# The router's high rows written by ACT straight from x3, the full rows by DVE, in a two-layer gated transformer kernel

## The reference

```python
x = x + jnp.tanh(g_xattn[0]) * _L0_xattn_ref(_layernorm(x), ctx_2048)            # fp8-like product
x = x + jnp.tanh(g_ffn[0]) * _L0_ffn_ref(_layernorm(x), L0_ffn_weight, ...)      # ternary weights
x = x + jnp.tanh(g_xattn[1]) * _L1_xattn_ref(_layernorm(x), ctx_2048, ctx_2048)  # 8 heads, softmax
x = x + jnp.tanh(g_ffn[1]) * _L1_ffn_ref(_layernorm(x), router_w, Wa, Wb)        # 8 experts, top 2
```

## Time and profile before

| | us |
|---|---|
| median of 3 runs | 2216.24 (2215.17 to 2216.98) |
| the profiled execution, its own time | 2218.67 |
| its span, first to last instruction | 2216.9 |
| PE busy | 1866.9 (84%) |
| DVE busy | 1668.4 (75%) |
| ACT busy | 1360.1 (61%) |
| POOL busy | 858.3 (39%) |

### The profile page before, as it was taken

How to read it: one execution, slowest core, us unless ns; L and a number is a source line. 1 busy time by engine, 2 the same in 40 slices (tenths; PEclk the granted TensorE clock), 3 DMA queues, 4 the chain that set the end, 5 groups by cost and what they waited for, 6 DMA issues and landing times.

```text
span 2216.9 us, 26479 instructions
## 1 busy us (share of the span) xinstructions
PE 1866.9 (84%) x8716; PEld 826.1 (37%) x8716; DVE 1668.4 (75%) x2348; ACT 1360.1 (61%) x2587; POOL 858.3 (39%) x1256
## 2 busy tenths in 40 slices
PE   0186667777746999999999999999999999999997
PEld 0032223332312444444444444444444444444443
DVE  8999989999546777777767777777777767777661
ACT  5798969977225565565565565565565565565650
POOL 2666646654023333333333433333333333433320
PEclk9998887898967999999999999999999999999998
DMA  7778769978637778878888878788778878778781
GB/s 217 193 208 198 199 176 233 250 182 213 183 92 140 150 154 170 159 156 168 158 156 165 161 162 163 158 162 161 161 155 168 158 156 163 164 163 163 133 150 41
DMA packets 963529, 369.33 MB, mean 167 GB/s; under 512 B 915136, under 2 KB 931520, under 8 KB 963392
## 3 DMA queue, kind: packets, MB, share of 16 engines
q1 hardware_dynamic: 963392, 367.64, 76.7%
HBM read 105.42 MB, written 33.55 MB: 63 GB/s over the span
## 4 chain that ended last, share of the span: by engine, by line
DVE 38%; issue 17%; ACT 16%; PE 13%; POOL 9%; DMA 6%; SPq 1%; POOLq 0%; ACTq 0%; DVEq 0%
ACT slot L716 7%; DVE tiny L971 7%; DVE tiny L1240 7%; POOL tiny L572 4%; ACT arena L708 4%; DMA slot<-slot 3%; POOL tiny L570 3%; DVE slot L1244 3%; ACT tiny L702 2%; PE accs L848 2%; PE sc L865 2%; PE accs L850 2%; PE accs L849 2%; DMA probs<-slot 2%; DVE slot L1022 2%
## 5 line engine op out<-in xcount | busy, mean ns | idle before, releaser
L1244 DVE SCALAR_TENSOR_TENSOR slot<-arena,tiny,slot 128x1024 f16<-128x1024 f32 x256 | 328.2, 1282 | 283.2 <-ACT slot L716 283.1
L865 PE MATMUL sc<-arena,slot 128*128 128x512 f16 x1536 | 381.3, 385 | 31.0 <-ACT arena L708 21.3
L716 ACT ACTIVATE slot<-arena,tiny 128x1024 f16<-128x1024 f32 x256 | 293.7, 1147 | 182.0 <-POOL tiny L572 166.6
L570 POOL TENSOR_SCALAR tiny<-tiny 128x1 f32<-128x1 f32 x256 | 99.3, 388 | 704.5 <-ACT arena L708 704.5
L1240 DVE TENSOR_REDUCE tiny<-sc 128x1 f32<-128x1024 f32 x256 | 308.5, 1206 | 57.8 <-PE sc L865 57.8
L708 ACT ACTIVATE arena<-sc,tiny,head_tab 128x1024 f32<-128x1024 f32 x256 | 308.4, 1205 | 8.6
L702 ACT ACTIVATE tiny<-tiny,head_tab 128x1 f32<-128x1 f32 x256 | 74.1, 289 | 359.4 <-DVE tiny L1240 358.4
L810 PE MATMUL sc<-probs,slot 128*128 128x512 f16 x768 | 190.0, 412 | 89.1 <-DMA slot<-slot 78.9
L865 PEld LDWEIGHTS sc<-arena,slot 128*128 128x128 f16 x1536 | 151.2, 99 | 219.7 <-ACT arena L708 25.9
L810 PE MATMUL sc<-wa_hi,slot 128*128 128x512 f16 x512 | 145.8, 406 | 78.1 <-DMA wa_lo<-wb_lo 46.8
L848 PE MATMUL accs<-wb_hi,slot 128*128 128x512 f16 x512 | 195.1, 381 | 7.5 <-DMA slot<-slot 7.5
(11 more groups left out here) (178 smaller groups left out, 3181.0 us busy)
## 6 DMA issues: line engine op xcount, KB each, us to landing
wb_hi<-in_ctx SPq DMA_DIRECT2D x36, 512.0 KB, 4.7
arena<-in_x SPq DMA_DIRECT2D x32, 512.0 KB, 3.6
x_scratch<-arena SPq DMA_DIRECT2D x32, 512.0 KB, 3.1
slot<-x_scratch SPq DMA_DIRECT2D x32, 512.0 KB, 3.8
slot<-in_ctx SPq DMA_DIRECT2D x32, 512.0 KB, 4.1
out<-arena SPq DMA_DIRECT2D x32, 512.0 KB, 3.4
slot<-in_L_ffn_weight SPq DMA_DIRECT2D x16, 512.0 KB, 3.4
slot<-in_L_ffn_Wa SPq DMA_DIRECT2D x16, 512.0 KB, 4.8
```

Source lines behind the costliest of these rows:

```text
L716: act.activation(PH[c % 2], PF[c % 2], ACT.Identity, scale=rinv[c % 2][:]).then_inc(s_ph.sem, 1)
L865: mm = pe.matmul(sc[:, c % 2, h * HALF:(h + 1) * HALF], q[i][:, c * P:(c + 1) * P], k[j][:, h * HALF:(h + 1) * HALF], start=start, stop=stop)
L1244: dve.scalar_tensor_tensor(out=PL[c % 2], in0=PF[c % 2], scalar=rinv[c % 2][:], in1=PH[c % 2], op0=ALU.mult, op1=ALU.subtract).then_inc(s_ ...
```

## The change

`rows_full` moves from ACT to DVE. There it waits for two of POOL's three factors (it subtracts the mean mv4 itself and multiplies by rs4, so it needs no nb4) and for `hidden_low` of the tile before, which reads T4. `rows_high` on ACT no longer copies T4: it reads x3 itself, with nb4 as bias and rs4 as scale, and writes float16. It waits for all three factors and for the transposed hidden rows of the tile before. `rows_low` waits for both. In ACT's order rows_high stands ahead of exp 2, where the two instructions stood behind it; in DVE's order rows_full stands behind row_maxima 2 and rows_low ahead of row_maxima 3.

```diff
@@ ACT @@
-            def rows_full(n):
-                act.wait_ge(l4_p.sem, l4_p.at(n))
-                act.activation(T4[:], X3[n % 2], ACT.Identity, bias=nb4[:], scale=rs4[:]).then_inc(l4_t.sem, 1)
-
             def rows_high(n):
-                act.wait_ge(l4_t.sem, l4_t.at(n))
+                act.wait_ge(l4_p.sem, l4_p.at(n))
                 after(act, h_turned, n - 1)
-                act.copy(T4HL[0], T4[:]).then_inc(l4_hi.sem, 1)
+                act.activation(T4HL[0], X3[n % 2], ACT.Identity, bias=nb4[:], scale=rs4[:]).then_inc(l4_hi.sem, 1)
@@ ACT's order @@
                 if nxt:
                     query_high(n + 1)
+                if prev:
+                    rows_high(n - 1)
                 if cur:
                     exp(n, 2)
-                if prev:
-                    rows_full(n - 1)
-                    rows_high(n - 1)
-                if cur:
                     prob_high(n, 2)
@@ DVE @@
+            def rows_full(n):
+                dve.wait_ge(l4_p.sem, l4_p.at(n, 2))
+                after(dve, h_lo, n - 1)
+                dve.tensor_scalar(T4[:], X3[n % 2], mv4[:, 0:1], rs4[:], ALU.subtract, ALU.mult).then_inc(l4_t.sem, 1)
+
             def rows_low(n):
                 dve.wait_ge(l4_hi.sem, l4_hi.at(n))
+                dve.wait_ge(l4_t.sem, l4_t.at(n))
                 dve.tensor_tensor(T4HL[1], T4[:], T4HL[0], ALU.subtract).then_inc(l4_lo.sem, 1)
@@ DVE's order @@
                 if cur:
                     row_maxima(n, 2)
+                if prev:
+                    rows_full(n - 1)
                 if before:
                     finish_x4(n - 2, 0)
+                if prev:
+                    rows_low(n - 1)
                 if cur:
                     row_maxima(n, 3)
-                if prev:
-                    rows_low(n - 1)
-                if cur:
                     prob_low(n, 2)
```

More of the change, by code:

```diff
@@ L726, in query_high, with rows_high @@
                 act.copy(QHL[n % 2][0], T3[:]).then_inc(l3_hi.sem, 1)
-            def rows_full(n):
+            def rows_high(n):
                 act.wait_ge(l4_p.sem, l4_p.at(n))
-                act.activation(T4[:], X3[n % 2], ACT.Identity, bias=nb4[:], scale=rs4[:]).then_inc(l4_t.sem, 1)
-            def rows_high(n):
-                act.wait_ge(l4_t.sem, l4_t.at(n))
                 after(act, h_turned, n - 1)
-                act.copy(T4HL[0], T4[:]).then_inc(l4_hi.sem, 1)
+                act.activation(T4HL[0], X3[n % 2], ACT.Identity, bias=nb4[:], scale=rs4[:]).then_inc(l4_hi.sem, 1)
             def router_exp(n):
@@ L1331, in _ @@
                     row_maxima(n, 2)
+                if prev:
+                    rows_full(n - 1)
                 if before:
                     finish_x4(n - 2, 0)
-                if cur:
-                    row_maxima(n, 3)
                 if prev:
@@ L1338, in _ @@
                 if cur:
+                    row_maxima(n, 3)
                     prob_low(n, 2)
```

## The result

The changed kernel took 2234.82 us (median of 4 runs, 2232.81 to 2235.55) beside 2216.61 for the kernel before: a ratio of 1.0087 (95% interval 1.0073 to 1.0100), 18 us or 0.9% slower. Its profiled execution took 2235.16 us over a span of 2233.3.

A forecast was written before the change was run, and what follows sets the result against it. The softmax chain was taken to bound the kernel, PE's router wait being slack. Profiled 2218.67 + 28.8 (31 x 0.93) - 0.6 - 4.5 = 2242.4 us, 2.4 above the median of the runs, so 2240 us; range 2217 to 2258.

The forecast's parts named there:

- What bounds: Ordinary pass of 46.88 us: set by the softmax chain over DVE, ACT and POOL; PE's router wait is slack.
- Rival 1: PE's router wait sets the pace; 1.4 us per pass goes as rows land earlier: 2164 us, chance 0.12.
- nb4 held by rows_full: POOL's nb4 held by DVE's rows_full starting just before it, ending 0.47 us later; bounds 0 to 1.0 us.
- Rival 2: No lock on POOL's nb4, so a pass grows 0.46 us instead of 0.93: 2225 us, chance 0.20.
- rows_high ahead of exp 2, the cover of the factor gone: ACT, chunk 2: 1.23 us rows_high delays exp 2, POOL's factor is no longer hidden; prob_low 2 comes 0.93 us later.
- rows_low and row_maxima 3 cost nothing: DVE: row_maxima 3 ends about 1421.5, ACT wants it at 1422.7; costs nothing until 1.2 us of further delay.
- The last tile: Last tile, no softmax beside it: the path through the rows is shorter, -0.6 us.
- The long passes: Passes about 1.5 us longer after PE's clock falls behind long router waits; part of six falls would cost less.
- the term of -4.5 us: Half of 6 x 1.5 = 9 us for PE's clock falls, taken as given back.
- PE's idle time in several places: PE's 2.3 us idle per pass spreads over several places instead of the router alone, so clock falls cost less.
- Rival 3: PE's idle time gathers in one place, the clock falls each pass, 37 us more: 2277 us, chance 0.10.

The follow-up runs named there:

- experiment 1: The changed kernel with rows_full on DVE waiting for all three of POOL's factors, so nb4 runs first: 2218.53 us, ratio 1.0023 to the kernel before.
- experiment 8: The changed kernel with PE's router also waiting for DVE's quantise_full, gathering PE's idle time ahead of the router: 2236.43 us, ratio 1.0090 to the kernel before.
- Experiment 3: The changed kernel's instructions in the old order, rows_high behind exp 2 and rows_low behind row_maxima 3: 2187.09 us, ratio 0.9883 to the kernel before.
- 6: Changed instructions in the old places, row_norm behind row_factor 3, and quantise_full behind prob_low 3: 2198.17 us, ratio 0.9921 to the kernel before.
- 5: Changed instructions in the old places, with POOL's row_norm behind row_factor 3 instead of ahead: 2177.87 us, ratio 0.9832 to the kernel before.
- 2: The changed kernel with rows_full written as a DVE instruction with two SBUF inputs, which takes longer: 2250.85 us, ratio 1.0164 to the kernel before.
- 4: The kernel before with only places changed: rows_full and rows_high on ACT ahead of exp 2, rows_low ahead of row_maxima 3: 2254.29 us, ratio 1.0183.
- experiment 7: The kernel before with rows_full cut into eight ACT instructions of 128 columns: 2305.37 us, ratio 1.0411 to the kernel before.

## Why the prediction was right, point by point

- **What bounds.** Right. The softmax chain sets the ordinary pass and PE's wait at the router is slack. With the router's rows 1.6 us earlier the pass grew. Rival 1 (PE's wait sets the pace) is out.
- **nb4 held by rows_full.** Right in kind and size: 0.52 us for the 0.47 taken. rows_full took 0.81, not 0.75. Rival 2 is the kernel of experiment 1.
- **rows_high ahead of exp 2, the cover of the factor gone.** Right: 1.24 us for the 1.23 taken, and a wait of 1.00 us behind exp 2. In all 0.99 for the 0.93 forecast, pass 47.85 for 47.8. rows_low and row_maxima 3 cost nothing, as said.
- **The last tile.** Right. From POOL's L545 (end) to rows_low: 2175.25 - 2172.50 = 2.75 us before, 2192.08 - 2189.88 = 2.20 after, -0.55 for the -0.6 forecast.
- **The long passes.** The way is right and the size wrong: the term of -4.5 us, half of six clock falls, measured -11.3 over 28 passes. The falls alone gave back 8.2 of it (8.4 before, 0.2 after), and that the late transposes cost 3.1 us less was not in the sum at all. The prediction's reason, PE's idle time in several places, is borne out in part: behind the two longest transposes of the changed kernel the router's wait was 1.0 and 1.1 us and no fall came, and gathered again (experiment 8) the idle time brought ten falls. But two other things took part. There were fewer long waits to begin with, since only two transposes were that late instead of six. And PE stands 2.6 us earlier against the chain, where a fall costs little (0.3 us in experiment 8). How much is due to each isn't shown. Experiment 3 says that the late transposes alone don't bring the falls: it has six as late as before, but waits of 1.1 to 1.6 us at the router behind them, and one fall.
- **Rival 3**, the idle time in one place, is out for the changed kernel: its 2.0 to 2.3 us lie in up to three places, about 0.9 at the router, 1.05 at scores 7 and the rest at values. Experiment 8 shows that even gathered, at the router, it would have cost 2 us, not the 37 I gave it.

The sum with measured terms: 31 x 0.99 = +30.7, -0.6, -11.3 = +18.8 us. The medians differ by 18.2, but that nearness is partly luck: the terms are read from the two profiled executions, which differ by 16.5 (2235.16 and 2218.67). The 2.3 us too many lie at the start of the loop. The finish_x2 that opens the 28 passes stands at 741.8 us before and 741.5 after, so the passes up to there had not become longer in sum, and 31 was too many. The forecast of 2240 us was 5 too high mainly because the long passes gave back 6.8 us more than I took; mainly for the same reason rival 2 came out at 2218.5 instead of 2225, though its 0.46 us per pass was right (0.47).

## What to carry to other kernels

An engine's only wait need not be the bottleneck: follow the chain piece by piece through an ordinary pass. If it never touches the busiest engine, a wait that vanishes there buys nothing, while here 1 us added to the chain made every ordinary pass 1 us longer. Before moving work to DVE, look which small POOL instruction becomes ready at the same moment, and let the small one go first; here one extra wait was worth 14 us. And take form and place of a change apart: the same instructions in their old places were 1.2% faster instead of 0.9% slower, and 1.7% with one more POOL step moved.

## What the runs showed that I had not expected

**Tiny instructions in a row pay the lock one by one.** In experiment 3 row_norm, four instructions with 1.2 us of work, took 4.4 us beneath back-to-back DVE instructions; three of the four were held. Which of two lengths a pass had, 45.85 or 46.34, went with a start of rows_low on DVE that was 0.08 us later or earlier.

**A late transpose often has an instruction packet beside it.** Of the 256 transposes of the softmax of the kernel before, 28 took at least 5.5 us to land and 206 under 5. In 21 of the 28 the instruction queue moved a packet within 4.4 us after the issue; of the 206 usual ones, in 33. In the changed kernel it was 15 of 16, and 31 of 221. The one that makes a pass long at 1345 us (ACT waits for it ahead of prob_high 7), its landing and the DMA queues in its time:

```profile
DMA to landing us min/median/max: 6.1/6.1/6.1
```

```profile
q1 hardware_dynamic: 2747, 0.70, 98.9%
q8 instruction: 1, 0.02, 1.0%
```

ACT waits in every pass for one transpose, that of chunk 5, ahead of prob_high 7. Before, it landed late (5.9 to 6.2 us) in six passes, and in the same six in experiment 3. In the changed kernel it is slow in these six passes too, but in four of them it lands in 5.1 to 5.3 us. Waits over 2 us for it: six before and in experiment 3, four in 6, three in 5, two in the changed kernel and in 1, 2 and 4, one in 7 and 8. The early rows_high is thus not all of it, since experiment 7 has the old order. The same passes in different versions fit a fetch that comes at its own points of an engine's program and meets the transpose more or less fully, depending on the length of the pass. It was not tried: no run moved the fetches alone, so the packet as the cause, and why the long waits became fewer, stay open.
